# Moving the readout multiply of a selective scan from VectorE to GpSimd

## The chip, the cores and the metric

The kernel runs on all 8 cores of one Trainium2 chip. The metric is the device time of the slowest core in microseconds (us); lower is better. Each core works alone on its own half of a sequence and runs the same program, and no core waits for another.

## The reference

The input `x` is 4 sequences of 2048 steps with 4096 channels, in fp32. The layer is a selective scan (Mamba style) with 16 states per channel, a layer norm, an int8 quantized matrix product of 4096 by 4096, and another layer norm:

```python
A = -jnp.exp(A_log)                                   # 4096 x 16
xp = jnp.einsum('bld,rd->blr', x, x_proj_w)           # 128 + 16 + 16 columns
dt_in, B, C = xp[..., :128], xp[..., 128:144], xp[..., 144:]
dt = softplus(jnp.einsum('blr,dr->bld', dt_in, dt_proj_w) + dt_proj_b)
dA = jnp.exp(dt[..., None] * A)
dBx = dt[..., None] * B[:, :, None, :] * x[..., None]
h = dA_t * h + dBx_t                                  # scan over the steps
y = jnp.einsum('bdn,bn->bd', h, C_t)                  # sum over the 16 states
y = y + D * x
x = layernorm(x + y)
x = layernorm(x + quantized_matmul(x, W))
```

The change concerns the product `h * C` inside the sum over the 16 states.

## The kernel before

The host gives each core one half of one sequence (1024 steps, L) and the 1024 steps ahead of it (P; zeros for a first half). Everything is one program with five blocks of work after another. Each engine has its own queue and runs it in order. The queues are tied by semaphores whose values are counted while the program is built: `m_v` counts VectorE's finished instructions, `m_s` ScalarE's, `m_t` TensorE's, and `m_l0`, `m_l1`, `m_ld` and `m_st` count DMAs. The profile calls TensorE PE, VectorE DVE, ScalarE ACT, GpSimd POOL and the queue that issues the DMAs SP.

1. Transposes of `x` and quantization of the weight, stored to HBM.
2. The projections, then `dt` and `u = dt * x`, stored to HBM as `dt_st` and `u_st`; `D * x` is stored as `gd_st`.
3. The scan over the preceding 1024 steps (`ch == 0`). It is needed only for the state that it hands on (`carry`).
4. The scan over the core's own 1024 steps (`ch == 1`). The change is here.
5. Layer norm, the quantized product and the second layer norm.

Block 4 loops over 32 channel tiles (`dt`, 128 channels each on the 128 partitions). For each it takes the 16 states `n` in 4 groups of NQ = 4 (`q0`, and `k` in a group). All operands lie in one large bf16 tensor in SBUF, `slab`, each row of it 1024 elements long. For each state the engines do this:

- ScalarE: `dA = exp(dt * A)` (L653), into one of eight buffers.
- VectorE: B, `dBx = u * B` (L675), into one of two buffers; T, the scan (`tensor_tensor_scan`, L683), which reads `dA` and `dBx` and writes `h` into one of two buffers (by `k % 2`); C, `g = h * C` (L692), into one of four buffers (`o_g + k * L`).
- TensorE: two matmuls of 512 columns with the identity (L729), which add `g` into the PSUM tile `py0`. In this way the sum over the states is formed.

The order on VectorE is written out by hand with the helper `emit`, which waits for the named results, issues the instruction and notes its count in `ack`. For one group it is B0, B1, T0, T1, C0, B2, C1, B3, T2, T3, C2, C3. T2 has to wait for C0 and T3 for C1, because they write over the `h` buffers that C0 and C1 read. C(k) waits until TensorE has read `g` buffer k of the group before.

Before the groups of a channel tile, TensorE puts `D * x` into `py0` (L573). After them VectorE waits for the last matmul and copies `py0` to `slab` at `o_gd` (CAST, L740), and SP stores it (L745). The tile `gd` of the next channel tile goes into the same place (L549), so that SP waits for that copy and for its store before it issues this load. Both B0 and ScalarE's first exp of the next channel tile wait for this load (one semaphore counts it with the loads of `dt` and `u`).

GpSimd has no work in the loops; its only instruction in the program text is a wait for the output at the end.

Of the kernel before, what the change touches and what calls it, by code (L numbers as in the profile page):

```python
# [11 lines left out]
OP = mybir.AluOpType  # L12
# [3 lines left out]
def _build(D, P, L, N, R):  # L16
    assert R == 128 and D % 512 == 0 and P % 128 == 0 and P == L
    QL = 512 if L % 512 == 0 else L
    T = P + L
# [11 lines left out]
    nc = bass.Bass("TRN2", target_bir_lowering=False)  # L31
# [37 lines left out]
    with ExitStack() as _es:  # L69
        def _e(cm):  # L70
            return _es.enter_context(cm)
        slab = _e(nc.sbuf_tensor("slab", [128, SLAB], BF16))
# [24 lines left out]
        m_ld = _e(nc.semaphore("m_ld"))  # L97
        m_st = _e(nc.semaphore("m_st"))
        m_v = _e(nc.semaphore("m_v"))
        m_s = _e(nc.semaphore("m_s"))  # L100
        m_t = _e(nc.semaphore("m_t"))
# [5 lines left out]
        m_t2 = _e(nc.semaphore("m_t2"))  # L107
        m_st2 = _e(nc.semaphore("m_st2"))
        m_l2 = _e(nc.semaphore("m_l2"))
        blk = _e(nc.Block())  # L110
        o_dtwT = max(5 * T + L, 3 * D)
        dtwT = slab[:, o_dtwT : o_dtwT + nD * 128]
# [3 lines left out]
        xpwT = slab[:, o_xpwT : o_xpwT + nD * XP]  # L116
        assert o_xpwT + nD * XP <= SLAB - 2 * D
        C = {"ld": 0, "st": 0, "v": 0, "s": 0, "t": 0, "o": 0, "l0": 0, "l1": 0,
             "v2": 0, "s2": 0, "t2": 0, "st2": 0, "l2": 0}
        SEM = {"ld": m_ld, "st": m_st, "v": m_v, "s": m_s, "t": m_t, "o": m_o,  # L120
               "l0": m_l0, "l1": m_l1, "v2": m_v2, "s2": m_s2, "t2": m_t2,
               "st2": m_st2, "l2": m_l2}
        m_l = [m_l0, m_l1]

        def inc(instr, key, n=1):
            instr.then_inc(SEM[key], n)
            C[key] += n
# [19 lines left out]
        @blk.sync  # L147
        def _(sy):
            src = bass.AP(A_log.tensor, 0, [[N, 128], [128 * N, nD], [1, N]])
            sy.dma_start(out=A_sb[:, 0 : nD * N], in_=src).then_inc(m_ld, 16)  # L150
            sy.dma_start(out=dtb_sb[:], in_=bass.AP(dtb.tensor, 0, [[1, 128], [128, nD]]), allow_slow_non_contiguous=True).then_inc(m_ld, 16)
            sy.dma_start(out=Dv_sb[:], in_=bass.AP(D_vec.tensor, 0, [[1, 128], [128, nD]]), allow_slow_non_contiguous=True).then_inc(m_ld, 16)
            sy.dma_start(out=ident[:], in_=ident_in[:]).then_inc(m_ld, 16)
            sy.dma_start(out=fb[:], in_=xpw[0:128, :]).then_inc(m_ld, 16)
            sy.dma_start(out=fc[0:32, :], in_=xpw[128:XP, :]).then_inc(m_ld, 16)
            C["ld"] += 6 * 16
# [323 lines left out]
        NQ = 4  # L480
        o_br = 0
        o_cr = o_br + N * P
        o_dA = o_cr + N * L
        o_dbx = o_dA + 8 * P
        o_h = o_dbx + 2 * P
        o_g = o_h + 2 * P
# [15 lines left out]
        for ch in range(2):  # L502
# [21 lines left out]
            for dt in range(nD):  # L524
# [53 lines left out]
                for q0 in range(0, N, NQ):  # L578
# [63 lines left out]
                    else:  # L642
# [13 lines left out]
                        @blk.vector  # L656
                        def _(v, dt=dt, q0=q0, qb=qb, o_ut_=o_ut_):
                            s_last = C["s"]
                            if q0 == 0:
                                v.wait_ge(m_l[dt % 2], C["l%d" % (dt % 2)])  # L660
                                v.wait_ge(m_ld, C["ld"])
                            ack = {}
                            def emit(tag, wait_tags, fn):
                                for w in wait_tags:
                                    wv = ack.get(w) if isinstance(w, str) else w
                                    if wv:
                                        v.wait_ge(m_v, wv)
                                i = fn()
                                i.then_inc(m_v, 1)
                                C["v"] += 1  # L670
                                ack[tag] = C["v"]
                            def B(k):
                                n = q0 + k
                                pb_ = o_dbx + (k % 2) * P
                                return v.tensor_tensor(slab[:, pb_ : pb_ + P],  # L675
                                                       slab[:, o_ut_ : o_ut_ + P],
                                                       slab[:, o_br + n * P : o_br + (n + 1) * P],
                                                       OP.mult)
                            def TT_(k):
                                n = q0 + k  # L680
                                pb_ = o_dbx + (k % 2) * P
                                ph_ = o_h + (k % 2) * P
                                return nc.vector.tensor_tensor_scan(  # L683
                                    slab[:, ph_ : ph_ + P], slab[:, qb + k * P : qb + (k + 1) * P],
                                    slab[:, pb_ : pb_ + P],
                                    carry[:, dt * N + n : dt * N + n + 1],
                                    OP.mult, OP.add)
                            def CM(k):
                                n = q0 + k
                                ph_ = o_h + (k % 2) * P  # L690
                                pg = o_g + k * L
                                return v.tensor_tensor(slab[:, pg : pg + L],  # L692
                                                       slab[:, ph_ : ph_ + P],
                                                       slab[:, o_cr + n * L : o_cr + (n + 1) * L],
                                                       OP.mult)
                            def TW(k):
                                v.wait_ge(m_s, s_last - (NQ - 1 - k))
                                return TT_(k)
                            def CW(k):
                                wv = C.get(("gt", k), 0)  # L700
                                if wv:
                                    v.wait_ge(m_t, wv)
                                return CM(k)
                            emit("B0", [C.get("pbx0", 0)], lambda: B(0))
                            emit("B1", [C.get("pbx1", 0)], lambda: B(1))
                            emit("T0", ["B0"], lambda: TW(0))
                            emit("T1", ["B1"], lambda: TW(1))
                            emit("C0", ["T0"], lambda: CW(0))
                            emit("B2", ["T0"], lambda: B(2))
                            emit("C1", ["T1"], lambda: CW(1))  # L710
                            emit("B3", ["T1"], lambda: B(3))
                            emit("T2", ["B2", "C0"], lambda: TW(2))
                            emit("T3", ["B3", "C1"], lambda: TW(3))
                            emit("C2", ["T2"], lambda: CW(2))
                            emit("C3", ["T3"], lambda: CW(3))
                            C["pbx0"] = ack["T2"]
                            C["pbx1"] = ack["T3"]
                            par = (q0 // NQ) % 2
                            for k in range(NQ):
                                C[("dA", par, k)] = ack["T%d" % k]  # L720
                                C[("g", k)] = ack["C%d" % k]
                        @blk.tensor
                        def _(t, dt=dt, q0=q0):
                            for k in range(NQ):
                                n = q0 + k
                                pg = o_g + k * L
                                t.wait_ge(m_v, C[("g", k)])
                                for qq in range(L // QL):
                                    i = t.matmul(py0[:, qq * QL : (qq + 1) * QL], ident[:],  # L729
                                                 slab[:, pg + qq * QL : pg + (qq + 1) * QL],  # L730
                                                 start=False, stop=(n == N - 1))
                                inc(i, "t")
                                C[("gt", k)] = C["t"]
# [33 lines left out]
        for half in range(nHALF):  # L767
            tts = list(range(half * TTH, (half + 1) * TTH))
# [303 lines left out]
```

## Time and profile before

| | |
|---|---|
| median of 3 runs | 7538.08 us (7532.69 to 7562.11) |
| the profiled execution | 7583.93 us |
| its span on the slowest core (core 5) | 7582.4 us |
| spans of the 8 cores | 7513.1 to 7582.4 us |
| busy share of the span on core 5 | DVE 49%, ACT 20%, PE 19%, POOL 0% |
| block 4 on core 5 | about 2.07 ms, from 3937 us to 6006 us |

The span runs from the first to the last instruction of a core. A row of the trace's timeline has the start in us, the duration in us, the engine, the line of the kernel, the operation, output and inputs, and how many instructions are merged in it. In brackets stands how long the engine was idle before it and what ended that idle time. Instructions of one engine overlap a little: the distance from start to start is shorter than the duration. A row that groups a line has a count, the busy time in us and the mean duration in ns, and then the idle time of the engine before these instructions.

### The profile page before, as it was taken

To read this page: it belongs to the slowest core of one execution; us is meant where nothing else is said; L and a number is where in the kernel's file an instruction comes from. 1 tells how busy PE (TensorE), PEld (TensorE's weight loads), DVE (VectorE), ACT (ScalarE), POOL (GpSimd) and SP (SyncE) were. 2 spreads that over 40 slices of the span, in tenths; PEclk is the share of its full clock that TensorE was granted. 3 is DMA by queue.
4 is the path that set the end of the run, shared out by engine and by line. 5 is a ranking of instruction groups with operands and counts; after the bars stand their busy time and mean duration, and the time that the engine had idled before them with its cause. 6 is when DMAs were issued, how large, how long until landed. Compare 5 with 4: busy or idle time off the path is not lost.

```text
span 7582.4 us, 27156 instructions; the slowest of 8 cores (7513.1 to 7582.4 us)
## 1 busy us (share of the span) xinstructions
PE 1461.9 (19%) x5664; PEld 545.3 (7%) x5664; DVE 3693.3 (49%) x4200; ACT 1520.4 (20%) x1258; POOL 0.2 (0%) x4
## 2 busy tenths in 40 slices
PE   1010000100005210000002222222222225601651
PEld 0000000000001000000000000000000012201220
DVE  1222222222220117999968888888888740034002
ACT  0000000000000334555532222222222210011001
POOL 0000000000000000000000000000000000000000
PEclk9999999999997555555555555555555557755775
DMA  2455545555456441000030000000000133243233
GB/s 55 66 67 73 67 76 67 72 70 65 75 66 170 153 164 46 17 17 20 17 51 17 17 17 17 17 17 17 17 17 13 50 105 95 80 130 104 87 100 114
DMA packets 450787, 474.66 MB, mean 63 GB/s; under 512 B 263936, under 2 KB 349952, under 8 KB 446240
## 3 DMA queue, kind: packets, MB, share of 16 engines
q1 hardware_dynamic: 450624, 472.93, 28.7%
q14 instruction: 115, 0.94, 0.0%
q8 instruction: 48, 0.79, 0.0%
HBM read 330.10 MB, written 142.75 MB: 62 GB/s over the span
## 4 chain that ended last, share of the span: by engine, by line
issue 26%; DMA 22%; DVE 20%; PE 12%; SPq 10%; ACT 8%; DVEq 1%; ACTq 0%
PE ps_big L917 6%; SPq L221 5%; ACT slab L653 3%; DMA slab<-wq_st 3%; DVE slab L675 3%; DMA fd<-x_all 3%; DMA fc<-W 2%; DMA fa<-x_all 2%; SPq L292 2%; DMA gd_st<-slab 2%; DVE st L231 2%; DMA slab<-gd_st 2%; DMA f16a<-f_st 2%; PE ps_tr L272 2%; DMA slab<-xT_st 2%
## 5 line engine op out<-in xcount | busy, mean ns | idle before, releaser
L683 DVE TENSOR_TENSOR_SCAN slab<-slab,carry 128x1024 bf16<-128x1024 bf16 x512 | 1174.3, 2335 | 0.0
L653 ACT ACTIVATE slab<-slab,A_sb 128x1024 bf16<-128x1024 bf16 x512 | 556.4, 1139 | 1550.7 <-DMA slab<-gd_st 1218.2
L729 PE MATMUL py<-slab,ident_sb 128*128 128x512 bf16 x1024 | 497.6, 614 | 1283.0 <-DVE slab L692 1283.0
L590 ACT ACTIVATE slab<-fc,bias,A_sb 128x1024 bf16<-128x1024 f32 x512 | 583.0, 1227 | 438.0 <-DVE bias L564 438.0
L621 DVE SCALAR_TENSOR_TENSOR slab<-slab 128x1024 bf16<-128x1024 bf16 x512 | 604.9, 1218 | 6.7 <-ACT slab L590 6.7
L917 PE MATMUL ps_big<-slab 128*128 128x512 bf16 x2048 | 478.9, 399 | 326.1 <-DMA slab<-wq_st 326.1
L675 DVE TENSOR_TENSOR slab<-slab 128x1024 bf16<-128x1024 bf16 x512 | 339.8, 684 | 271.9 <-DMA slab<-gd_st 271.9
L932 DVE TENSOR_TENSOR fc<-ps_big,wsrep 128x512 f32<-128x512 f32 x64 | 39.7, 684 | 769.0 <-PE ps_big L917 769.0
L272 PE MATMUL ps_tr<-ident_sb,slab 128*128 128x128 bf16 x1024 | 129.3, 305 | 1349.5 <-DVE slab L264 1257.9
L692 DVE TENSOR_TENSOR slab<-slab 128x1024 bf16<-128x1024 bf16 x512 | 335.1, 675 | 0.0
L613 DVE TENSOR_TENSOR slab<-slab 128x1024 bf16<-128x1024 bf16 x512 | 329.6, 684 | 0.6 <-DVE bias L564 0.4
L247 ACT ACTIVATE wsrep<-fb,st 128x4096 f32<-128x4096 f32 x16 | 59.3, 3707 | 1319.5 <-DVE st L241 1319.5
L231 DVE TENSOR_REDUCE st<-fc 128x1 f32<-128x4096 f32 x16 | 70.7, 4420 | 502.2 <-DMA fc<-W 502.2
L573 PE MATMUL py<-slab,ident_sb 128*128 128x512 bf16 x64 | 32.4, 609 | 1353.4 <-DMA slab<-gd_st 1353.4
L917 PEld LDWEIGHTS ps_big<-slab 128*128 128x128 bf16 x2048 | 207.4, 102 | 597.2 <-issue 379.0
L247 ACT ACTIVATE wsrep<-fc,st 128x4096 f32<-128x4096 f32 x16 | 59.3, 3707 | 795.4 <-DVE st L241 795.4
L729 PEld LDWEIGHTS py<-slab,ident_sb 128*128 128x128 bf16 x1024 | 84.8, 110 | 1695.8 <-issue 1678.8
L231 DVE TENSOR_REDUCE st<-fb 128x1 f32<-128x4096 f32 x16 | 70.7, 4420 | 269.4 <-DMA fb<-W 269.4
L940 ACT ACTIVATE slab<-fc,asc 128x512 f16<-128x512 f32 x64 | 40.9, 709 | 799.5 <-DVE fc L932 799.5
L272 PEld LDWEIGHTS ps_tr<-ident_sb,slab 128*128 128x128 bf16 x1024 | 98.9, 137 | 1380.0 <-issue 1380.0
L459 DVE TENSOR_TENSOR slab<-slab 128x2048 bf16<-128x2048 bf16 x32 | 39.2, 1226 | 310.9 <-ACT slab L448 310.9
L326 PE MATMUL ps_tr<-ident_sb,slab 128*128 128x128 bf16 x512 | 64.7, 305 | 578.4 <-DVE slab L317 533.1
(89 smaller groups left out, 1503.4 us busy)
## 6 DMA issues: line engine op xcount, KB each, us to landing
slab<-wq_st SPq DMA_DIRECT2D x64, 1024.0 KB, 10.8
slab<-xT_st SPq DMA_DIRECT2D x96, 512.0 KB, 3.6
fb<-W SPq DMA_DIRECT2D x128, 256.0 KB, 7.4
wq_st<-slab SPq DMA_DIRECT2D x32, 1024.0 KB, 16.1
fc<-W SPq DMA_DIRECT2D x128, 256.0 KB, 19.1
fa<-x_all SPq DMA_DIRECT2D x32, 512.0 KB, 21.2
xT_st<-slab SPq DMA_DIRECT2D x16, 1024.0 KB, 7.9
fd<-x_all SPq DMA_DIRECT2D x32, 512.0 KB, 22.8
```

Of the source, the lines that this page charges most:

```text
L221: i = sy.dma_start(out=wb[:, ck * wck : (ck + 1) * wck], in_=W[jt * 128 : (jt + 1) * 128, ck * wck : (ck + 1) * wck])
L231: i = v.reduce_max(st[:, sp : sp + 1], wb[:], axis=AX.X, apply_absolute_value=True)
L272: i = t.matmul(ps_tr[:, 1024 + k * 128 : 1024 + (k + 1) * 128], slab[:, o_pwa + dt * 128 : o_pwa + (dt + 1) * 128], ident[:], is_transpose ...
L590: sfin(s.activation(slab[:, qb + k * P : qb + (k + 1) * P], fc[:, 0:P], AF.Exp, scale=A_sb[:, dt * N + n : dt * N + n + 1], bias=bias16[:, ...
L613: return v.tensor_tensor(slab[:, pb_ : pb_ + P], slab[:, o_ut_ : o_ut_ + P], slab[:, o_br + n * P : o_br + (n + 1) * P], OP.mult)
L621: return nc.vector.scalar_tensor_tensor(slab[:, ph_ : ph_ + P], slab[:, pb_ : pb_ + P], 1.0, slab[:, qb + k * P : qb + (k + 1) * P], OP.mu ...
L653: sfin(s.activation(slab[:, qb + k * P : qb + (k + 1) * P], slab[:, o_dt_ : o_dt_ + P], AF.Exp, scale=A_sb[:, dt * N + n : dt * N + n + 1]))
L675: return v.tensor_tensor(slab[:, pb_ : pb_ + P], slab[:, o_ut_ : o_ut_ + P], slab[:, o_br + n * P : o_br + (n + 1) * P], OP.mult)
L683: return nc.vector.tensor_tensor_scan(slab[:, ph_ : ph_ + P], slab[:, qb + k * P : qb + (k + 1) * P], slab[:, pb_ : pb_ + P], carry[:, dt ...
L692: return v.tensor_tensor(slab[:, pg : pg + L], slab[:, ph_ : ph_ + P], slab[:, o_cr + n * L : o_cr + (n + 1) * L], OP.mult)
L729: i = t.matmul(py0[:, qq * QL : (qq + 1) * QL], ident[:], slab[:, pg + qq * QL : pg + (qq + 1) * QL], start=False, stop=(n == N - 1))
L917: i = t.matmul(ps_ffn[toff], slab[:, o_xqT + dt * (128 * TTH) + toff * 128 : o_xqT + dt * (128 * TTH) + (toff + 1) * 128], slab[:, o_wgb + ...
```

## The change

C leaves VectorE's queue and becomes a `tensor_tensor` on GpSimd with the same operands. A new semaphore `m_p` counts GpSimd's results. GpSimd waits for the scan T(k) of its state and for TensorE's reading of the `g` buffer; TensorE waits for `m_p` in place of `m_v`; T(k) waits for the GpSimd multiply that reads the `h` buffer it is going to write. VectorE's order in a group becomes B0, B1, T0, T1, B2, B3, T2, T3. T2 and T3 wait for C0 and C1 of the same group, and T0 and T1 for C2 and C3 of the group before.

```diff
@@ VectorE, one group @@
-                            def CM(k):
-                                n = q0 + k
-                                ph_ = o_h + (k % 2) * P
-                                pg = o_g + k * L
-                                return v.tensor_tensor(slab[:, pg : pg + L],
-                                                       slab[:, ph_ : ph_ + P],
-                                                       slab[:, o_cr + n * L : o_cr + (n + 1) * L],
-                                                       OP.mult)
+                            p_base = C["p"]
                             def TW(k):
                                 v.wait_ge(m_s, s_last - (NQ - 1 - k))
+                                if k < 2:
+                                    wv = C.get("hC%d" % k, 0)
+                                    if wv:
+                                        v.wait_ge(m_p, wv)
+                                else:
+                                    v.wait_ge(m_p, p_base + (k - 2) + 1)
                                 return TT_(k)
-                            def CW(k):
-                                wv = C.get(("gt", k), 0)
-                                if wv:
-                                    v.wait_ge(m_t, wv)
-                                return CM(k)
                             emit("B0", [C.get("pbx0", 0)], lambda: B(0))
                             emit("B1", [C.get("pbx1", 0)], lambda: B(1))
                             emit("T0", ["B0"], lambda: TW(0))
                             emit("T1", ["B1"], lambda: TW(1))
-                            emit("C0", ["T0"], lambda: CW(0))
                             emit("B2", ["T0"], lambda: B(2))
-                            emit("C1", ["T1"], lambda: CW(1))
                             emit("B3", ["T1"], lambda: B(3))
-                            emit("T2", ["B2", "C0"], lambda: TW(2))
-                            emit("T3", ["B3", "C1"], lambda: TW(3))
-                            emit("C2", ["T2"], lambda: CW(2))
-                            emit("C3", ["T3"], lambda: CW(3))
+                            emit("T2", ["B2"], lambda: TW(2))
+                            emit("T3", ["B3"], lambda: TW(3))
                             C["pbx0"] = ack["T2"]
                             C["pbx1"] = ack["T3"]
+                            C["hC0"] = p_base + 3
+                            C["hC1"] = p_base + 4
                             par = (q0 // NQ) % 2
                             for k in range(NQ):
                                 C[("dA", par, k)] = ack["T%d" % k]
-                                C[("g", k)] = ack["C%d" % k]
+                                C[("tts", k)] = ack["T%d" % k]
+                        @blk.gpsimd
+                        def _(g, dt=dt, q0=q0):
+                            if dt == 0 and q0 == 0:
+                                g.wait_ge(m_ld, C["ld"])
+                            for k in range(NQ):
+                                n = q0 + k
+                                ph_ = o_h + (k % 2) * P
+                                pg = o_g + k * L
+                                g.wait_ge(m_v, C[("tts", k)])
+                                wv = C.get(("gt", k), 0)
+                                if wv:
+                                    g.wait_ge(m_t, wv)
+                                i = g.tensor_tensor(slab[:, pg : pg + L],
+                                                    slab[:, ph_ : ph_ + P],
+                                                    slab[:, o_cr + n * L : o_cr + (n + 1) * L],
+                                                    OP.mult)
+                                inc(i, "p")
@@ TensorE, one group @@
-                                t.wait_ge(m_v, C[("g", k)])
+                                t.wait_ge(m_p, C["p"] - (NQ - 1 - k))
```

## Rows read from the trace of the kernel before

**Rows 1.** The page: the span, and busy time of each engine.

```profile
span 7582.4 us, 27156 instructions; the slowest of 8 cores (7513.1 to 7582.4 us)
PE 1461.9 (19%) x5664; PEld 545.3 (7%) x5664; DVE 3693.3 (49%) x4200; ACT 1520.4 (20%) x1258; POOL 0.2 (0%) x4
```

**Rows 2.** Busy time in windows, blocks 3 to 5; columns as the first line says.

```profile
core 5: us, PE busy (x) PEld busy (x) DVE busy (x) ACT busy (x) POOL busy (x), PEclk, DMA share, GB/s
2880.00:3930.00 1050.00, 0.00 (x0) 0.00 (x0) 978.52 (x1600) 583.03 (x512) 0.00 (x0) 0.50 0.10 24
3930.00:6010.00 2080.00, 530.01 (x1088) 89.12 (x1088) 1806.92 (x1568) 556.38 (x512) 0.00 (x0) 0.50 0.06 17
6010.00:7583.00 1573.00, 543.58 (x2560) 256.86 (x2560) 341.75 (x368) 136.38 (x136) 0.00 (x0) 0.65 0.32 103
```

**Rows 3.** Groups by line in 3930 to 6010 us, block 4.

```profile
L683 DVE TENSOR_TENSOR_SCAN slab<-slab,carry 128x1024 bf16<-128x1024 bf16 x512 | 1174.3, 2335 | 0.0
L653 ACT ACTIVATE slab<-slab,A_sb 128x1024 bf16<-128x1024 bf16 x512 | 556.4, 1139 | 1550.7 <-DMA slab<-gd_st 1218.2 <-DVE slab L683 329.7
L729 PE MATMUL py<-slab,ident_sb 128*128 128x512 bf16 x1024 | 497.6, 614 | 1283.0 <-DVE slab L692 1283.0
L675 DVE TENSOR_TENSOR slab<-slab 128x1024 bf16<-128x1024 bf16 x512 | 339.8, 684 | 271.9 <-DMA slab<-gd_st 271.9
L692 DVE TENSOR_TENSOR slab<-slab 128x1024 bf16<-128x1024 bf16 x512 | 335.1, 675 | 0.0
L740 DVE CAST slab<-py 128x1024 bf16<-128x1024 f32 x32 | 39.2, 1225 | 48.5 <-PE py L729 48.5
```

**Rows 4.** Timeline, 4510 to 4526 us: one group of four states.

```profile
4510.96 1.29 DVE L675 TENSOR_TENSOR slab<-slab 128x1024 bf16<-128x1024 bf16 x2 [6.34 <-DMA slab<-gd_st]
...
4512.18 4.59 DVE L683 TENSOR_TENSOR_SCAN slab<-slab,carry 128x1024 bf16<-128x1024 bf16 x2
4516.69 0.67 DVE L692 TENSOR_TENSOR slab<-slab 128x1024 bf16<-128x1024 bf16 x1
4517.27 0.69 DVE L675 TENSOR_TENSOR slab<-slab 128x1024 bf16<-128x1024 bf16 x1
...
4517.87 0.68 DVE L692 TENSOR_TENSOR slab<-slab 128x1024 bf16<-128x1024 bf16 x1
4518.47 0.69 DVE L675 TENSOR_TENSOR slab<-slab 128x1024 bf16<-128x1024 bf16 x1
...
4518.70 1.01 PE L729 MATMUL py<-slab,ident_sb 128*128 128x512 bf16 x2 [0.19 <-DVE slab L692]
4519.08 4.59 DVE L683 TENSOR_TENSOR_SCAN slab<-slab,carry 128x1024 bf16<-128x1024 bf16 x2
...
4525.97 4.59 DVE L683 TENSOR_TENSOR_SCAN slab<-slab,carry 128x1024 bf16<-128x1024 bf16 x2
```

**Rows 5.** Timeline, 4500 to 4511 us: the end of one channel tile.

```profile
4500.61 1.26 DVE L692 TENSOR_TENSOR slab<-slab 128x1024 bf16<-128x1024 bf16 x2
...
4501.42 1.87 PE L729 MATMUL py<-slab,ident_sb 128*128 128x512 bf16 x4 [4.68 <-DVE slab L692]
...
4503.39 1.23 DVE L740 CAST slab<-py 128x1024 bf16<-128x1024 f32 x1 [1.52 <-PE py L729]
4504.70 0.32 SPq L745 DMA_DIRECT2D y_st<-slab  x1
...
4506.94 0.32 SPq L549 DMA_DIRECT2D slab<-gd_st  x1
```

**Rows 6.** Groups of GpSimd (POOL) by line, the whole span.

```profile
L31 POOL MEMSET const-bfloat16-1.0<- 128x1 bf16 x1 | 0.1, 102 | 0.0
```

**Rows 7.** The page's groups: a two-input product in fp32, one input in PSUM.

```profile
L932 DVE TENSOR_TENSOR fc<-ps_big,wsrep 128x512 f32<-128x512 f32 x64 | 39.7, 684 | 769.0 <-PE ps_big L917 769.0
```

**Rows 8.** L683 by itself: duration ns min/median/max, first and last start us.

```profile
L683 DVE TENSOR_TENSOR_SCAN slab<-slab,carry x512: 2315/2334/2354, 3938.5 to 5997.7; 128x1024 bf16<-128x1024 bf16 x171
```

More of the change, by code:

```diff
@@ L109, in _build @@
         m_l2 = _e(nc.semaphore("m_l2"))
+        m_p = _e(nc.semaphore("m_p"))
         blk = _e(nc.Block())
@@ L118, in _build @@
         C = {"ld": 0, "st": 0, "v": 0, "s": 0, "t": 0, "o": 0, "l0": 0, "l1": 0,
-             "v2": 0, "s2": 0, "t2": 0, "st2": 0, "l2": 0}
+             "v2": 0, "s2": 0, "t2": 0, "st2": 0, "l2": 0, "p": 0}
         SEM = {"ld": m_ld, "st": m_st, "v": m_v, "s": m_s, "t": m_t, "o": m_o,
                "l0": m_l0, "l1": m_l1, "v2": m_v2, "s2": m_s2, "t2": m_t2,
-               "st2": m_st2, "l2": m_l2}
+               "st2": m_st2, "l2": m_l2, "p": m_p}
         m_l = [m_l0, m_l1]
```

## The prediction

> **What bounds the kernel now.** I read the page first. VectorE (DVE) has the most work, 3693 of 7582 us, and GpSimd (POOL) has four instructions in all [rows 1]. A mean over the whole span says little, so I read the blocks next. Block 4, where the change is, lasts 2080 us in its window, and VectorE is busy for 1807 us of them; in block 5 it is busy for 342 of 1573 us [rows 2]. So VectorE is the bound of block 4, and block 4 alone.
>
> The groups by line say how its time is made up. For each of 512 states (32 channel tiles by 16) there are one B at 684 ns, one T at 2335 ns and one C at 675 ns. In front of T and C VectorE never idles, and in front of B only 272 us in all, for the load of `gd` [rows 3]. ScalarE is busy 556 us and TensorE 530 us, both far below.
>
> The timeline gives the start-to-start price, which is what VectorE's queue pays. Two scans take 4.51 us (4512.18 to 4516.69), so T is 2.25. A pair C, B takes 1.20 (4517.27 to 4518.47), so each is 0.60. A whole group goes from 4512.18 to 4525.97, 13.79 us [rows 4]. The sum agrees: 4 x 2.25 + 8 x 0.60 = 13.8. There are 128 groups, 1765 us.
>
> The rest of block 4 is 32 ends of a channel tile. From the end of the last scan (C2 starts at 4500.61) the order is C2, C3, the last matmuls, the CAST, the store, the load of `gd` at 4506.94 [rows 5], and B0 at 4510.96 [rows 4]. That is 10.3 us from C2 to B0, in which VectorE is idle for most.
>
> **The change, part by part.**
>
> *C leaves VectorE.* Four instructions of 0.60 leave each group: 13.79 - 2.39 = 11.4 us. That is a gain of at most 2.39 x 128 = 306 us, and only if nothing else holds the scans up.
>
> *C on GpSimd, its price G.* The trace has no GpSimd instruction with work in it, only sets of one column in 0.10 us [rows 6]. So G has to be bounded. From below I take ScalarE's pass over the same 1024 columns with one input, 1.14 us [rows 3]. From above: the plain two-input product that runs slowest per element is 684 ns for 512 [rows 7], 1.34 ns each; an engine that takes its two operands one after the other would need twice that, 1024 x 2.67 = 2.74 us. In between lies the scan, the slowest instruction of this loop for 1024 columns of two inputs, 2.34 us. A programmable engine that must step over both inputs is nearest to that, and I take G = 2.34 us. The Trainium skill, GPSIMD Engine Reference, section on performance versus the Vector engine, gives 4497 ns for a two-input fp32 add of 2048 columns; if half of it, about 2.25 us, held here, the sum below would be 46 us smaller. No row here shows it.
>
> *The new waits of VectorE.* T2 waits for C0, T3 for C1, the next T0 and T1 for C2 and C3. Behind a waiting T stand, in order, the other scans and B's, and behind these ScalarE, whose exp wants the `dA` buffers back, and TensorE. If GpSimd works freely beside VectorE, C0 has the time of T1, B2 and B3 before T2 needs it: 2.25 + 1.20 = 3.45 us. With G = 2.34 and a handover of 0.15 us (C1 ends at 4518.55, its matmul starts at 4518.70 [rows 4]) this is hidden. GpSimd's own work would be 4 x 2.34 = 9.4 us in an 11.4 us group.
>
> *Whether they work beside each other.* This decides the sign. Every VectorE instruction of the group, B and T, reads two operands of `slab`, and so does C on GpSimd. If an instruction of one engine has to wait while the other reads, there is no overlap at all. The group is then everything in line: 11.4 for B and T, 4 x 2.34 = 9.36 for C, and handovers. VectorE runs ahead until T2 lacks C0, then C0 and C1 run, then T2 and T3 and the next B0 and B1, then C2 and C3: four handovers of 0.15, 0.6 us. Together 21.4 us against 13.79, plus 7.6; times 128 that is 970 us. The ends of the channel tiles change little: their C2 and C3 are in this sum, and the CAST still follows the last matmul by 0.10 us [rows 5].
>
> The trace cannot settle it. It shows that operands of the same memory do not disturb each other as such: the scan's duration stays within 2315 and 2354 ns over 512 instances [rows 8], while ScalarE writes and TensorE reads `slab` beside it. It shows nothing of GpSimd. Beside VectorE's two operands it has only engines that read one each, ScalarE and TensorE's moving operand [rows 3]; a second engine that wants two more streams has no example. For that reason I take turns for likelier than free overlap. The Trainium skill, SBUF — State Buffer, section with the single rule on the shared port pair, says that VectorE takes its second SBUF input through a read interface that it shares with GpSimd, that an instruction with two SBUF inputs therefore contends with a GpSimd instruction that reads SBUF, and that this is an exclusive lock for the whole instruction. By that rule the group is the 21.4 us in line, and without it at most the freely overlapped 11.4. No run here shows it yet; it speaks against this change.
>
> *TensorE and ScalarE.* TensorE's pair of matmuls takes 1.0 us for each C, of 2.85 to 5.3 us per state, so it stays hidden, at the granted clock of 0.50 that it has already in this window [rows 2]. ScalarE needs 4 x 1.14 in a group. Neither costs anything. The blocks 1 to 3 and 5 hold no edit; block 5 only starts later.
>
> *The sum.* The profiled execution was 7583.93 us on 7582.4 of span: 7584 + 970 = 8554. That execution lies 46 us above the median of the runs (7538), so the median comes to 8508 us, +12.9%.
>
> **The rivals.**
>
> *Free overlap.* The two engines read beside each other. Then VectorE stays the bound with 11.4 us a group, minus 306 us. The end of each channel tile grows: now the CAST starts 2.8 us after the last scan (4500.61 to 4503.39 [rows 5]); afterwards it is 0.15 + 2.34 for C3, 0.15, 1.01 for the matmuls and 0.10, 3.75 us, and C2 still runs about 0.2 us when T3 ends; together plus 1.2 us, 32 times 37 us. Net minus 269 us: median 7269. For it: VectorE is clearly the bound, GpSimd is empty, and the wait is covered by 3.45 us. Against it: it needs two readers of two operands each at full speed. It decides at G: above 3.45 us less a handover, 3.3 us, GpSimd would be the slower of the two.
>
> *GpSimd slow, yet free.* At twice the scan, G = 4.7 us, GpSimd bounds the group with 18.8 us, plus 5.0; times 128, plus 641, and plus 1.2 + 2.4 at 32 ends, 115: median about 8290. Not excluded by any row, but G is twice what I take.
>
> *Half-way.* The engines share rather than take turns, so that each is stretched while the other reads. The group is then between 11.4 and 21.4 us. The middle, 16.4 us, gives plus 334, median about 7870. Break-even is a group of 13.5 us, with the longer ends, so only a small part of it is not slower.
>
> *Turns with a cheap C.* With turns, break-even is 4 G + 0.6 = 2.39, G = 0.45 us, which is less than VectorE's own 0.60. So turns mean slower whatever G is: at G = 1.14 the group is 16.6 us, plus 354, median 7890; at 2.74 it is 23.0, plus 1175, median 8713.
>
> **How the numbers follow.** Turns get 0.70; a slow but free GpSimd 0.04; half-way 0.10, of which 0.07 slower, 0.02 same and 0.01 faster; free overlap 0.16, of which 0.15 faster and 0.01 same. Slower by over 0.5% is thus 0.81, within 0.5% 0.03, faster 0.16; 0.5% is about what a measurement of this kernel can tell from no change. The predicted time is that of turns, 8508. The range of the turns alone by the bounds of G is 7890 to 8713; handovers that were underestimated by 0.15 us each would add 77 more. With most of half-way and the slow GpSimd, which fall into it, 7800 to 8800 leaves out about 2 in 10, nearly all of it free overlap.
>
> **What the profile after would show.** Right: block 4 lasts about 3040 us; POOL has 512 products, and two that follow each other start about 2.3 us apart; during a stretch of C no B or T proceeds, and VectorE's idle time (or its stretched durations, if an instruction that waits for the reader counts as running) is about half of block 4; TensorE waits for GpSimd and no longer for VectorE. B and T take 11.4 us in a group once the stretches are taken out. Blocks 1 to 3 and 5 keep their lengths.
>
> Wrong: scans at 2.25 us start to start with a C running beside them at the same time (free overlap, a group of 11.4 us); POOL busy without gaps at 4 or more us each with VectorE waiting (slow and free); scans and C's both stretched by a part (half-way). If G is near 1.1 us with turns, the mechanism is right and the size is off by 600 us.

## The result, and the profile after

| | before | after |
|---|---|---|
| median, 10 runs each, timed together | 7554.51 us | 8208.58 us |
| range of the runs | 7532.69 to 7578.06 | 8196.87 to 8231.0 |
| slowest span of the profiled execution | 7582.4 us | 8201.2 us |

The ratio is 1.087, with a 95% interval of 1.0852 to 1.0888: the change makes the kernel 8.7% slower, by 654 us. 8508 us (+12.9%) was predicted. The direction was right, and so was the cause, as the experiments below show; the size was too large by about 300 us.

The page of the kernel after, first its span and busy times, then its largest groups (busy us, mean ns | idle us before, by releaser):

```profile
span 8201.2 us, 27411 instructions; the slowest of 8 cores (8179.9 to 8201.2 us)
PE 1479.8 (18%) x5664; PEld 530.3 (6%) x5664; DVE 4238.7 (52%) x3688; ACT 1520.3 (19%) x1258; POOL 1640.7 (20%) x516
L727 POOL TENSOR_TENSOR slab<-slab 128x1024 bf16<-128x1024 bf16 x512 | 1640.5, 3223 | 4981.1 <-DVE slab L684 4981.1
L676 DVE TENSOR_TENSOR slab<-slab 128x1024 bf16<-128x1024 bf16 x512 | 1174.3, 2332 | 241.2 <-DMA slab<-gd_st 241.2
L684 DVE TENSOR_TENSOR_SCAN slab<-slab,carry 128x1024 bf16<-128x1024 bf16 x512 | 1173.2, 2330 | 0.3 <-DVE slab L676 0.3
L739 PE MATMUL py<-slab,ident_sb 128*128 128x512 bf16 x1024 | 517.9, 609 | 1926.7 <-POOL slab L727 1926.7
```

VectorE has lost 512 instructions, yet its busy time has risen from 3693 to 4239 us [rows 1]. The scans (now L684) are as they were, 2330 ns, with 0.3 us of idle time before them in all. The B's (now L676) carry all of it: the same instruction on the same shapes has gone from a mean of 684 ns [rows 3] to 2332 ns, which is 834 us more in the sum of 512. VectorE is not idle while it is held up. It counts as busy, in an instruction that does not get on. (Records of one engine overlap a little, so such sums are not exact.)

The windows of the kernel after, the blocks 3, 4 and 5 (columns as in [rows 2]):

```profile
2880.00:3930.00 1050.00, 1.01 (x2) 0.14 (x2) 979.30 (x1599) 586.10 (x517) 2.54 (x1) 0.50 0.10 24
3930.00:6640.00 2710.00, 549.32 (x1086) 74.22 (x1086) 2345.38 (x1052) 550.03 (x507) 1637.93 (x512) 0.50 0.04 13
6640.00:8202.00 1562.00, 542.05 (x2560) 256.47 (x2560) 342.26 (x368) 136.39 (x136) 0.00 (x0) 0.65 0.32 102
```

Block 3 has the VectorE time that it had, 979 us, and block 5 has 342 us, as before [rows 2], each at the granted clock that it had. All of the loss lies in block 4. From its first B to the end of its last CAST it took 2066.7 us before (3937.28 to 6003.94) and takes 2701 us now (3923.8 to 6624.8): 634 us more. The blocks before it took 13.5 us less and block 5 took 2 us less, so that the spans of the two profiled executions differ by 619 us. The medians differ by 654: the profiled execution of before lies 29 us above its median (7583.93 against 7554.51), that of after 6 below (8202.71 against 8208.58).

The timeline of the kernel after, from one pair of states to the next, all engines but ScalarE and the weight loads. The scans at its start are T2 and T3 of a group; the two instructions of L727 are C2 and C3, those of L676 are B0 and B1 of the next group, and the last row has its T0 and T1. The pair before it, T0 and T1 with B2 and B3 behind them, looks the same (4515.66 to 4525.16).

```profile
4525.16 4.58 DVE L684 TENSOR_TENSOR_SCAN slab<-slab,carry 128x1024 bf16<-128x1024 bf16 x2
...
4527.70 6.47 POOL L727 TENSOR_TENSOR slab<-slab 128x1024 bf16<-128x1024 bf16 x2 [3.02 <-DVE slab L684]
4529.66 5.06 DVE L676 TENSOR_TENSOR slab<-slab 128x1024 bf16<-128x1024 bf16 x2
...
4531.79 1.01 PE L739 MATMUL py<-slab,ident_sb 128*128 128x512 bf16 x2 [5.95 <-POOL slab L727]
...
4534.31 1.01 PE L739 MATMUL py<-slab,ident_sb 128*128 128x512 bf16 x2 [1.51 <-POOL slab L727]
4534.64 4.58 DVE L684 TENSOR_TENSOR_SCAN slab<-slab,carry 128x1024 bf16<-128x1024 bf16 x2
```

This is how to read it. T2 ends at about 4527.5, and C2 begins on GpSimd at 4527.70, by the record. T3 is not disturbed (both scans take their 4.58 us). But C2's result is there only at about 4531.65, just before its matmul starts at 4531.79 (the 0.15 us between them is the handover of [rows 4]): C2 has stood still until T3's end at 4529.7, and then took 1.9 us. In that time B0 stands still, although its record begins at 4529.66. Then B0 runs its 0.6 us while C3 waits, and C3 takes 1.9 us while B1 waits: the two matmuls start 2.52 us apart, 0.6 and 1.9. Behind the scans the engines change places after every instruction. So far this is a reading of the timeline; the experiments test it. A pair is 4534.64 - 4525.16 = 9.48 us, where it was 6.90 (4512.18 to 4519.08 [rows 4]). In numbers: 9.48 = 4.51 for the scans + 1.20 for the B's + 2 x 1.89. So a C costs VectorE 1.89 us on GpSimd, and cost it 0.60 on VectorE itself.

### The profile page after: what moved, and what is told of

The parts are those of the page before. It is cut to its first block, busy times and chain, and to the rows that moved or that the text cites. A ratio compares the mean times of both kernels' runs of the same rounds, so it can differ in the third digit from the quotient of the medians.

```text
span 8201.2 us, 27411 instructions; the slowest of 8 cores (8179.9 to 8201.2 us)
## 1 busy us (share of the span) xinstructions
PE 1479.8 (18%) x5664; PEld 530.3 (6%) x5664; DVE 4238.7 (52%) x3688; ACT 1520.3 (19%) x1258; POOL 1640.7 (20%) x516
## 4 chain that ended last, share of the span: by engine, by line
issue 35%; DMA 20%; DVE 17%; PE 10%; SPq 9%; ACT 6%; POOL 2%; DVEq 1%; ACTq 0%; POOLq 0%
PE ps_big L927 6%; SPq L222 4%; DMA slab<-wq_st 2%; DMA fc<-W 2%; DMA fd<-x_all 2%; DMA fa<-x_all 2%; SPq L293 2%; DMA gd_st<-slab 2%; DVE st L232 2%; POOL slab L727 2%; DVE slab L684 2%; PE ps_tr L273 2%; DMA slab<-xT_st 2%; DVE slab L622 1%; ACT wsrep L248 1%
## 5 line engine op out<-in xcount | busy, mean ns | idle before, releaser
L727 POOL TENSOR_TENSOR slab<-slab 128x1024 bf16<-128x1024 bf16 x512 | 1640.5, 3223 | 4981.1 <-DVE slab L684 4981.1
L676 DVE TENSOR_TENSOR slab<-slab 128x1024 bf16<-128x1024 bf16 x512 | 1174.3, 2332 | 241.2 <-DMA slab<-gd_st 241.2
L684 DVE TENSOR_TENSOR_SCAN slab<-slab,carry 128x1024 bf16<-128x1024 bf16 x512 | 1173.2, 2330 | 0.3 <-DVE slab L676 0.3
L739 PE MATMUL py<-slab,ident_sb 128*128 128x512 bf16 x1024 | 517.9, 609 | 1926.7 <-POOL slab L727 1926.7
L273 PE MATMUL ps_tr<-ident_sb,slab 128*128 128x128 bf16 x1024 | 129.3, 305 | 1346.5 <-DVE slab L265 1254.9
L614 DVE TENSOR_TENSOR slab<-slab 128x1024 bf16<-128x1024 bf16 x512 | 330.3, 687 | 0.6 <-DVE bias L565 0.4
L574 PE MATMUL py<-slab,ident_sb 128*128 128x512 bf16 x64 | 32.4, 609 | 1323.1 <-DMA slab<-gd_st 1323.1
L282 DVE COPY slab<-ps_tr 128x1024 bf16<-128x1024 bf16 x128 | 88.6, 692 | 162.9 <-PE ps_tr L273 162.9
```

The costliest lines, as they stand in the source:

```text
L273: i = t.matmul(ps_tr[:, 1024 + k * 128 : 1024 + (k + 1) * 128], slab[:, o_pwa + dt * 128 : o_pwa + (dt + 1) * 128], ident[:], is_transpose ...
L614: return v.tensor_tensor(slab[:, pb_ : pb_ + P], slab[:, o_ut_ : o_ut_ + P], slab[:, o_br + n * P : o_br + (n + 1) * P], OP.mult)
L676: return v.tensor_tensor(slab[:, pb_ : pb_ + P], slab[:, o_ut_ : o_ut_ + P], slab[:, o_br + n * P : o_br + (n + 1) * P], OP.mult)
L684: return nc.vector.tensor_tensor_scan(slab[:, ph_ : ph_ + P], slab[:, qb + k * P : qb + (k + 1) * P], slab[:, pb_ : pb_ + P], carry[:, dt ...
L727: i = g.tensor_tensor(slab[:, pg : pg + L], slab[:, ph_ : ph_ + P], slab[:, o_cr + n * L : o_cr + (n + 1) * L], OP.mult)
L739: i = t.matmul(py0[:, qq * QL : (qq + 1) * QL], ident[:], slab[:, pg + qq * QL : pg + (qq + 1) * QL], start=False, stop=(n == N - 1))
```

## The experiments

Two theories stood from the start. *Turns*: a VectorE instruction and a GpSimd instruction exclude each other while both read `slab`. *Waits*: the scans' new waits for C hold VectorE up. A third was *sharing*: both are stretched while they run together. The times of before that go with each run were taken on the same chip.

The times of e1 to e4 rest on two runs each, that of e5 on ten, those of e6 to e8 on four. The diffs are shortened.

**e1_side.** The contention without any wait: C stays on VectorE, and GpSimd works for nobody.

```diff
 (the kernel before; after the scans of a group, on GpSimd:)
+    g.wait_ge(m_v, C[("tts", k)])
+    g.wait_ge(m_p, C["p"] - NQ + 1)          # its own store of four before
+    i = g.tensor_tensor(fdb[:, k * L : (k + 1) * L],
+                        slab[:, o_br + n * P : o_br + (n + 1) * P],
+                        slab[:, o_cr + n * L : o_cr + (n + 1) * L], OP.mult)
```

> The kernel before, with C on VectorE as it was, and beside it a GpSimd product of two constant rows of slab (B row times C row) into an unused tile, 512 times, each let go by one scan. Nobody waits for it before block 4 ends. It adds work and leaves out none. Turns (a two-input VectorE instruction and a reading GpSimd instruction exclude each other): each product holds VectorE up for about 1.9 us, which is what it did in the changed kernel; 512 x 1.9 = 970, so about 8500 us. Waits (VectorE lost its time only to the scans' new waits for C): nobody waits here, so no change, about 7550 us. Sharing (both are stretched): in between, with scans longer than 2.35 us.

Measured: 8485.03 us against 7537.27, ratio 1.127 (1.1204 to 1.1336). The waits are refuted: nobody waits for GpSimd here, and yet 948 us are lost, 1.85 us for each of the 512 products. The groups by line of this kernel, from 3960 to 6000 us:

```profile
L734 POOL TENSOR_TENSOR fd<-slab 128x1024 bf16<-128x1024 bf16 x348 | 1125.0, 3251 | 916.5 <-DVE slab L684 916.5
L684 DVE TENSOR_TENSOR_SCAN slab<-slab,carry 128x1024 bf16<-128x1024 bf16 x348 | 797.3, 2329 | 0.0
L693 DVE TENSOR_TENSOR slab<-slab 128x1024 bf16<-128x1024 bf16 x348 | 719.7, 2087 | 0.0
L676 DVE TENSOR_TENSOR slab<-slab 128x1024 bf16<-128x1024 bf16 x348 | 396.8, 1160 | 124.6 <-DMA slab<-gd_st 124.6
```

Here it is mostly VectorE's own C (L693, 675 ns before [rows 3]) that stands behind the second scan and carries the hold, 2087 ns: 1.41 us on C and 0.48 on B (1160 against 684), 1.89 together. The scan is again untouched. Who is held is whichever instruction of VectorE comes next.

**e2_memset and e3_copy.** What of GpSimd's instruction does it: the running, or the reading? All waits stay as in the changed kernel.

```diff
-    i = g.tensor_tensor(slab[:, pg : pg + L], slab[:, ph_ : ph_ + P],
-                        slab[:, o_cr + n * L : o_cr + (n + 1) * L], OP.mult)
+    i = g.memset(slab[:, pg : pg + L], 0.5)                        # e2_memset
+    i = g.tensor_copy(slab[:, pg : pg + L], slab[:, ph_ : ph_ + P])  # e3_copy
```

> The changed kernel with GpSimd's multiply replaced by a memset of g (writes 1024 columns, reads nothing); all waits are kept. The readout product is left out, so y is not the reference's. Turns between readers only: nothing of VectorE is held up, the group takes 11.4 us, 306 us less than before with a slightly longer end of each tile, about 7250 to 7290 us. Turns with any GpSimd instruction: 11.4 plus four memsets of perhaps 0.9 us, 15 us a group, about 7700 us. Waits: the memset is short enough to be covered, also about 7270 us.

> The changed kernel with GpSimd's multiply replaced by a copy of h to g, one input in place of two; all waits are kept. The multiplication by C is left out, so y is not the reference's. Turns: VectorE is held for each copy; if a copy takes half of the product's 1.9 us, the group is 11.4 + 4 x 0.95 = 15.2 us, 180 us more than before, about 7730 us, and B or T instructions show the hold. Waits or free overlap: a copy is covered by T1, B2 and B3, about 7270 us.

Measured: e2_memset 7255.35 us, ratio 0.9637 (0.9581 to 0.9693); e3_copy 7630.52 us, ratio 1.0135 (1.0071 to 1.0199). The copy's expectation was 100 us too high: it was put at 0.95 us of hold and has 0.81, as shown below. The timeline of e2_memset:

```profile
4525.15 1.27 DVE L676 TENSOR_TENSOR slab<-slab 128x1024 bf16<-128x1024 bf16 x2
4526.33 4.59 DVE L684 TENSOR_TENSOR_SCAN slab<-slab,carry 128x1024 bf16<-128x1024 bf16 x2
4530.83 1.27 DVE L676 TENSOR_TENSOR slab<-slab 128x1024 bf16<-128x1024 bf16 x2
4532.02 4.58 DVE L684 TENSOR_TENSOR_SCAN slab<-slab,carry 128x1024 bf16<-128x1024 bf16 x2
```

and its memsets in the timeline of GpSimd:

```profile
4525.41 0.95 POOL L727 MEMSET slab<- 128x1024 bf16 x1 [1.29 <-PE py L736]
4528.85 0.95 POOL L727 MEMSET slab<- 128x1024 bf16 x1 [2.50 <-DVE slab L684]
```

One memset runs from 4525.41 to 4526.36 right beside the two B's, one beside a scan, and each takes 0.95 us. The pair is 5.69 us, the 11.4 us a group of the free overlap. So GpSimd's memset, which only writes, takes no turns with these B's and scans, and the semaphores of the change cost nothing that this run can tell. With one input the holds are back. The timeline of VectorE in e3_copy:

```profile
4519.55 4.58 DVE L684 TENSOR_TENSOR_SCAN slab<-slab,carry 128x1024 bf16<-128x1024 bf16 x2
4524.05 2.90 DVE L676 TENSOR_TENSOR slab<-slab 128x1024 bf16<-128x1024 bf16 x2
4526.87 4.58 DVE L684 TENSOR_TENSOR_SCAN slab<-slab,carry 128x1024 bf16<-128x1024 bf16 x2
```

A pair is 7.32 us: 5.71 + 2 x 0.81. So one operand that GpSimd reads is enough for a hold. What a copy and a product take when nothing hinders them is the least duration of all 512, the copy in e3_copy and the product in the kernel after (duration ns min/median/max, first and last start us):

```profile
L727 POOL COPY slab<-slab x512: 1034/2018/2947, 3904.2 to 6040.5; 128x1024 bf16<-128x1024 bf16 x171
L727 POOL TENSOR_TENSOR slab<-slab x512: 2108/3085/4009, 3927.5 to 6620.2; 128x1024 bf16<-128x1024 bf16 x171
```

They cost VectorE 0.81 and 1.89 us: about 0.2 us of each passes beside VectorE's work.

**e4_h4.** The waits taken away in the changed kernel itself, by two more `h` buffers in a tile that block 4 leaves unused.

```diff
-    if k < 2:
-        wv = C.get("hC%d" % k, 0)            # C(k + 2) of the group before
-        if wv:
-            v.wait_ge(m_p, wv)
-    else:
-        v.wait_ge(m_p, p_base + (k - 2) + 1) # C(k - 2) of this group
+    wv = C.get("hC%d" % k, 0)                # C(k) of the group before
+    if wv:
+        v.wait_ge(m_p, wv)
-    slab[:, ph_ : ph_ + P]                   # two buffers
+    HB(k)                                    # four: two in slab, two in fd
```

> The changed kernel with four h buffers instead of two: a scan waits only for the C of four states before, so that T2 and T3 no longer wait for C0 and C1. Turns: the same work stays in line, group still about 19 us, about 8200 us (100 us either way, by another order of who goes first). Waits: with the waits gone VectorE runs at its 11.4 us a group, about 7290 us.

Measured: 8176.51 us, ratio 1.086 (1.0797 to 1.0924), where the change had 1.087. No gain that can be told. Its timeline of VectorE:

```profile
4515.27 4.58 DVE L690 TENSOR_TENSOR_SCAN slab<-slab,carry 128x1024 bf16<-128x1024 bf16 x2
4519.77 5.06 DVE L683 TENSOR_TENSOR slab<-slab 128x1024 bf16<-128x1024 bf16 x2
4524.75 4.58 DVE L690 TENSOR_TENSOR_SCAN fd<-slab,carry 128x1024 bf16<-128x1024 bf16 x2
```

The pair is 9.48 us as before the edit, with the B's held as they were. This is the second refutation of the waits.

**e5, e6, e7 and e8.** Now the other side: does it matter what VectorE's instruction reads? ScalarE can write `dA` to PSUM, so that the scan has one SBUF operand.

```diff
 (e5 on the kernel before, e6 on the changed one)
-    sfin(s.activation(slab[:, qb + k * P : qb + (k + 1) * P],
+    sfin(s.activation(ps_big[:, (k % 2) * P : (k % 2 + 1) * P],     # fp32, waits for T(n-2)
 ...
-    slab[:, ph_ : ph_ + P], slab[:, qb + k * P : qb + (k + 1) * P],
+    slab[:, ph_ : ph_ + P], ps_big[:, (k % 2) * P : (k % 2 + 1) * P],
 (e7: e6, and the order T, B, T, B; e8: this order, with dA left in SBUF)
+    if q0 == 0:
+        BW(0); BW(1)
+    for k in range(NQ):
+        emit("T%d" % k, [C[("Bn", k)]], lambda: TW(k))
+        if q0 + k + 2 < N:
+            BW(k + 2)                       # four dBx buffers
```

> A control without GpSimd: the kernel before, with one edit: ScalarE writes dA in fp32 into two PSUM buffers instead of eight bf16 buffers in SBUF, so that the scan T reads one operand from SBUF and one from PSUM. Both theories: the scan's 2.25 us start to start do not hang on where dA lies, and a state takes 3.45 us on VectorE against 1.14 on ScalarE, so two buffers are enough. About 7540 us, within 0.5% of before. If the scan is slower from PSUM, 0.06 us of it would be 30 us.

> The changed kernel with dA in PSUM as in the control. Turns only between two-SBUF-input instructions: the scan no longer takes turns, C0 runs beside T1; B2 starts when T1 ends, C1 gets in behind it and B3 is held for about 1.9 us, so half of the holds go: a pair takes 4.5 + 1.2 + 1.9 = 7.6 us, a group 15.2, 180 us more than before, about 7750 us. Turns with every VectorE instruction, whatever it reads: no change against the changed kernel, about 8200 us.

> e6 with VectorE's order changed to T, B, T, B (the B of two states ahead behind each scan, dBx in four buffers in the space that dA left). Turns only for two SBUF inputs: C(k) waits out one B of 0.6 us, then runs its 1.9 us inside the next scan of 2.25 us, which is no longer excluded; nothing is held. A state takes 2.25 + 0.60 = 2.85 us, a group 11.4, 306 us less than before, and 40 us come back at the ends of the tiles: about 7280 us. Turns with every instruction: about 8200 us.

> The order T, B, T, B of e7 with dA left in SBUF, dBx in four buffers of an unused tile: parts the order from the place of dA. Turns for two SBUF inputs: every T and B is excluded by a C again, 11.4 + 4 x 1.9 = 19 us a group, about 8200 us. If the order alone had helped, about 7280 us.

| | median, us | ratio to before | 95% interval |
|---|---|---|---|
| e5_before_dA_psum | 7527.10 | 1.0008 | 0.9992 to 1.0024 |
| e6_after_dA_psum | 7734.44 | 1.0273 | 1.0248 to 1.0297 |
| e7_dA_psum_order | 7292.38 | 0.9685 | 0.966 to 0.971 |
| e8_order_only | 8171.44 | 1.0851 | 1.0823 to 1.0878 |

e5 is the control: without work on GpSimd the place of `dA` is worth nothing. With C on GpSimd it takes the ratio from 1.087 to 1.0273. The timeline of e6:

```profile
4522.77 4.58 DVE L690 TENSOR_TENSOR_SCAN slab<-ps_big,carry,slab 128x1024 bf16<-128x1024 f32 x2
...
4525.31 4.64 POOL L736 TENSOR_TENSOR slab<-slab 128x1024 bf16<-128x1024 bf16 x2 [3.01 <-DVE slab L690]
4527.27 3.23 DVE L682 TENSOR_TENSOR slab<-slab 128x1024 bf16<-128x1024 bf16 x2
...
4527.57 1.01 PE L748 MATMUL py<-slab,ident_sb 128*128 128x512 bf16 x2 [4.12 <-POOL slab L736]
...
4530.42 4.58 DVE L690 TENSOR_TENSOR_SCAN slab<-ps_big,carry,slab 128x1024 bf16<-128x1024 f32 x2
```

C0 starts at 4525.31 and its matmul at 4527.57: it has run beside T1 without a halt. Only one hold is left, that of B3 by C1: the two B's take 3.23 us in place of 1.29 [rows 4], 1.94 more. A pair is 7.65 us (4522.77 to 4530.42). e7 takes away the last hold by order. Its timeline, one state:

```profile
4502.19 2.35 POOL L740 TENSOR_TENSOR slab<-slab 128x1024 bf16<-128x1024 bf16 x1 [0.49 <-DVE slab L690]
4502.48 2.34 DVE L690 TENSOR_TENSOR_SCAN slab<-ps_big,carry,slab 128x1024 bf16<-128x1024 f32 x1
...
4504.74 0.67 DVE L682 TENSOR_TENSOR slab<-slab 128x1024 bf16<-128x1024 bf16 x1
...
4505.03 2.35 POOL L740 TENSOR_TENSOR slab<-slab 128x1024 bf16<-128x1024 bf16 x1 [0.49 <-DVE slab L690]
4505.33 2.35 DVE L690 TENSOR_TENSOR_SCAN slab<-ps_big,carry,slab 128x1024 bf16<-128x1024 f32 x1
```

A product (4502.19 to 4504.54) is over before the next B (4504.74), the scan beside it keeps its 2.34 us, and a state takes 2.85 us on VectorE, exactly T and B. And the same order with `dA` in SBUF, e8, the timelines of VectorE and then GpSimd:

```profile
4528.55 0.66 DVE L681 TENSOR_TENSOR fd<-slab 128x1024 bf16<-128x1024 bf16 x1
4529.13 4.20 DVE L689 TENSOR_TENSOR_SCAN slab<-slab,carry,fd 128x1024 bf16<-128x1024 bf16 x1
4533.25 0.66 DVE L681 TENSOR_TENSOR fd<-slab 128x1024 bf16<-128x1024 bf16 x1
```

```profile
4528.83 2.35 POOL L739 TENSOR_TENSOR slab<-slab 128x1024 bf16<-128x1024 bf16 x1 [2.35 <-DVE slab L689]
```

The product takes the same 2.35 us as in e7, but now the scan is the one that is held, 4.20 us against 2.34. Reckoned back from its end at 4533.33, the scan got on at 4533.33 - 2.34 = 4530.99, 0.19 us before the product's record ends at 4531.18: this is where the 0.2 us of above lie. Between e7 and e8 `dA` has its place changed and `dBx` lies in another SBUF tile; the scan has two SBUF operands in e8 and one in e7. That is worth 879 us. One thing changed with the place: `dA` is fp32 in PSUM and bf16 in SBUF. No run has an fp32 `dA` in SBUF, so that the place is what counts, and not the type, is the likely reading and not shown by itself. e7 is faster than both kernels, by 3.15% against before.

## Why the prediction came out as it did

*VectorE is the bound of block 4, and the rest of the program only starts later*: right, by the windows.

*The waits*: the prediction had them hidden only if the engines overlap freely, and in the turns it let T2 wait for C0. They are hidden in the turns too. The scans idle 0.3 us in all, and e4 and e2 show no cost of the waits or of the semaphores.

*The engines take turns*: right, and it is the cause. e1 shows it without a wait, e2 and e3 show that GpSimd's reading is needed for it, and e5 to e8 that `dA` in SBUF as the scan's second SBUF operand is (with the reserve on its type). Sharing is out as well: in every timeline one instruction runs at full speed and the other stands, but for 0.2 us. The prediction spoke of a second engine that wants two more streams; by e3 one is enough. The Trainium skill, SBUF — State Buffer, section "Who interferes with whom", says just this, down to the GpSimd instruction that only writes; here the traces agree, with scans of 4.20 and 2.34 us. The exclusive lock for the whole instruction, which the prediction names from there, fits but for the 0.2 us. The order in which requests were served can be read in the timelines as well: C2, let go during T3 (4527.70), went ahead of the next B0, whose record begins at 4529.66.

*The order of the turns*: wrong, and it moves the sum only through the handovers. I let VectorE run on until T2 lacked C0. In fact each C gets in ahead of the next B, and so the holds stand on the B's, not on the scans.

*The size*: this is the term that was mis-sized, "G = 2.34 us" and its "four handovers of 0.15, 0.6 us". A C with its handover was put at 2.34 + 0.15 = 2.49 us and costs 1.89. Of these 0.60, 0.24 is G, which is 2.1 us (between my bounds; the halved figure of 2.25 that the prediction sets beside its own would have been nearer), 0.15 is the handover, of which the pair of 9.48 us shows nothing, and 0.21 passes beside VectorE's instruction, which the prediction did not have. Four times 0.60 is 2.4 us a group, times 128 is 307 us. The group was said to be 21.4 us and is 2 x 9.48 = 18.97. That the scan's duration was only a tenth off G is luck: it was taken by likeness, and no row ties the one to the other.

The rest of the account. The end of a channel tile before, from its last T2 to the next B0:

```profile
4496.11 4.58 DVE L683 TENSOR_TENSOR_SCAN slab<-slab,carry 128x1024 bf16<-128x1024 bf16 x2
...
4510.96 1.29 DVE L675 TENSOR_TENSOR slab<-slab 128x1024 bf16<-128x1024 bf16 x2 [6.34 <-DMA slab<-gd_st]
```

and after:

```profile
4497.79 4.58 DVE L684 TENSOR_TENSOR_SCAN slab<-slab,carry 128x1024 bf16<-128x1024 bf16 x2
...
4514.38 1.29 DVE L676 TENSOR_TENSOR slab<-slab 128x1024 bf16<-128x1024 bf16 x2 [5.54 <-DMA slab<-gd_st]
```

Before, a channel tile was 7 pairs of 6.90, 1.2 for the first two B's, and this end of 14.85. Now it is 7 pairs of 9.48, the same 1.2, and 16.6. That is 7 x 2.58 + 1.74 = 19.8 us a tile, times 32 is 634 us, what block 4 has gained. I had held the ends for nearly unchanged because I counted their C2 and C3 in the groups; sorted as here, they are 56 of the 634. Sorted as in the prediction, 970 less 307 is 663 us, and the other 30 are the load of `gd`: VectorE's idle time for it fell from 271.9 [rows 3] to 241.2 us. Why the load came sooner after the CAST stays open.

The free overlap that I priced as a rival at 269 us less, 7269, is about what e7 reaches once nothing is held: 231 us less than its own before, 7292. One limit in that rival was wrong: GpSimd would become the slower of the two where 4 G is more than the group's 11.4 us, above G = 2.85 us, and not above 3.3.

## What to carry to other kernels

Before work is moved from VectorE to GpSimd, count SBUF operands on both sides. In these runs, where the GpSimd instruction read SBUF and the VectorE instruction beside it read two SBUF operands, the two engines worked as one, and a product of 1024 columns that cost 0.6 us cost 1.9. Either take one operand of the long VectorE instruction from PSUM (here free, by e5, as ScalarE could write it there), and let the short ones with two SBUF operands fall where GpSimd is idle, or leave the work where it is. And look for a hold in the mean duration of a group whose shapes have not changed, not in idle time.

## What the runs showed of the hardware beyond that

The record of an instruction that is held takes in the time in which it is held, on both engines: B's of 2.5 us for 0.6 us of work on VectorE, C's with a mean of 3223 ns for about 2.1 us on GpSimd. The busy time of GpSimd in the kernel after, 1640 us, is by about a third waiting (512 x 2.1 = 1075). The Trainium skill, Perfetto Trace Analysis, section "GPSIMD Engine Instruction", warns that such spans are unreliable and wants the spacing of consecutive ones; at the end of a tile, where no B lies between, the matmuls of two C's start at 4504.42 and 4506.49, 2.07 us apart:

```profile
4504.42 1.01 PE L739 MATMUL py<-slab,ident_sb 128*128 128x512 bf16 x2 [5.95 <-POOL slab L727]
...
4506.49 1.01 PE L739 MATMUL py<-slab,ident_sb 128*128 128x512 bf16 x2 [1.06 <-POOL slab L727]
```

A scan that reads fp32 from PSUM and bf16 from SBUF takes as long as one that reads two bf16 operands from SBUF: 2335 ns in e5 (here from 3960 to 5600 us), 2335 before [rows 3].

```profile
L689 DVE TENSOR_TENSOR_SCAN slab<-ps_big,carry,slab 128x1024 bf16<-128x1024 f32 x406 | 931.1, 2335 | 0.0
```
